# Attention with a mixture of experts: last half batch reordered, gathers issued eight pairs ahead

## The reference

```python
x = L0_attn_x                                    # 4 x 1024 x 256, float32
x = x + layernorm(attention(layernorm(x)))       # 16 heads, 4 kv heads, rotary, causal
x = x + layernorm(ffn(layernorm(x)))
# ffn(x): 64 experts of width 96, 6 of them for each token
scores = sigmoid(x @ gate_w)                     # choice: best 4 of 8 groups, then best 6 experts
w      = scores[chosen] / sum(scores[chosen]) * 2.5
# each expert takes its first 128 * 6 * 2 * 2 / 64 = 48 tokens at most
routed = sum over chosen e of w * ((silu(x @ w_gate[e]) * (x @ w_up[e])) @ w_down[e])
shared = (silu(x @ ws_gate) * (x @ ws_up)) @ ws_down
ffn    = routed + shared
```

## Time and profile before

| | |
|---|---|
| time, median of 3 runs | 2049.85 us (2048.86 to 2051.9) |
| the profiled execution's own time | 2050.17 us |
| its span, first to last instruction | 2048.4 us |
| block `attention`, to | 1781 us of the span |
| block `last_quad`, from and to | 1781 to 1847.2 us |
| block `experts`, from and to | 1847.2 to 2048.4 us |
| PE, DVE, ACT, POOL busy over the span | 93, 65, 56, 63 per cent |

### The profile page before, as it was taken

One profiled execution on the slowest core, in us unless ns is written; L12 is line 12 of the kernel. 1 busy time (PEld: TensorE's weight loads), 2 busy tenths in 40 slices (PEclk: granted clock), 3 DMA queues, 4 the chain that ended last, 5 costly groups with the idle time before them and its releaser, 6 DMA issues. The chain is left out here.

```text
span 2048.4 us, 34361 instructions
## 1 busy us (share of the span) xinstructions
PE 1895.5 (93%) x11846; PEld 1566.2 (76%) x11846; DVE 1330.8 (65%) x3149; ACT 1154.0 (56%) x2632; POOL 1284.4 (63%) x1061
## 2 busy tenths in 40 slices
PE   5999999999999999999999999999999999787926
PEld 4888888888888888888888888888888888543412
DVE  5566666667767677777667667676676778762324
ACT  3556666666656665566565665666655655333413
POOL 5758576666666765758485766676666755214733
PEclk8999999999999999999999999999999999995658
DMA  5005000001110100000100100001101000298476
GB/s 178 16 27 164 29 21 6 22 6 31 48 52 6 42 1 22 11 27 32 58 21 6 42 6 27 6 21 57 32 6 42 1 17 17 105 357 284 67 220 210
DMA packets 77292, 120.22 MB, mean 59 GB/s; under 512 B 9639, under 2 KB 57717, under 8 KB 75873
## 3 DMA queue, kind: packets, MB, share of 16 engines
q1 hardware_dynamic: 65264, 92.61, 13.6%
q0 software_dynamic: 7248, 12.72, 2.6%
q10 hardware_dynamic: 4608, 12.68, 1.9%
HBM read 90.34 MB, written 38.53 MB: 63 GB/s over the span
## 5 line engine op out<-in xcount | busy, mean ns | idle before, releaser
L561 PE MATMUL s_ps<-kT,q 128*128 128x512 f32 (+3 forms) x2304 | 584.3, 371 | 13.9 <-POOL q L1136 7.9
L824 DVE TENSOR_TENSOR pT<-t_ps,pT 128x512 fp32r<-128x512 f32 (+3 forms) x768 | 401.0, 550 | 191.0 <-ACT pT L969 189.8
L811 DVE TENSOR_REDUCE neg_max<-s_ps 128x1 f32<-128x640 f32 (+7 forms) x512 | 384.6, 751 | 110.8 <-PE s_ps L561 103.9
L561 PEld LDWEIGHTS s_ps<-kT,q 128*128 128x128 f32 x2304 | 408.3, 192 | 61.6 <-ACT probs L958 11.6
L586 PE MATMUL av_ps<-pT,v 128*128 128x512 f32 x1728 | 442.2, 400 | 2.7 <-DVE pT L824 2.7
L1121 POOL TENSOR_TENSOR k_roped<-raw,sinT 64x512 f32<-64x512 f32 x316 | 406.7, 1287 | 24.3
L969 ACT ACTIVATE pT<-t_ps 128x512 fp32r<-128x512 f32 (+3 forms) x768 | 348.7, 490 | 129.8 <-PE t_ps L571 125.0
L958 ACT ACTIVATE probs<-s_ps,neg_max 128x640 f32<-128x640 f32 (+7 forms) x512 | 381.9, 746 | 63.3 <-DVE neg_max L811 61.0
L586 PEld LDWEIGHTS av_ps<-pT,v 128*128 128x128 f32 x1728 | 311.8, 189 | 67.1 <-DVE pT L824 7.8
L571 PE MATMUL t_ps<-k_ident,probs 128*128 128x128 f32 x2304 | 340.1, 274 | 11.6 <-DVE pT L824 7.9
L1118 POOL TENSOR_TENSOR k_roped<-raw,cosT 128x512 f32<-128x512 f32 x158 | 204.4, 1294 | 220.1 <-ACT raw L930 201.3
(11 more groups left out here) (245 smaller groups left out, 1877.4 us busy)
## 6 DMA issues: line engine op xcount, KB each, us to landing
w_early<-in_expert_w SPq DMA_DIRECT2D x5, 2560.0 KB, 26.6
w_early<-sums SPq DMA_DIRECT2D x24, 512.0 KB, 8.8
k_staged<-in_wpack SPq DMA_DIRECT2D x47, 256.0 KB, 2.9
sums<-sums ACTq DMA_DIRECT2D x2, 4144.0 KB, 22.9
k_staged<-in_wpack SPq DMA_DIRECT2D x16, 512.0 KB, 3.7
e_w_late<-in_expert_w SPq DMA_DIRECT2D x3, 2560.0 KB
k_xw<-in_x SPq DMA_DIRECT2D x4, 1024.0 KB, 5.8
k_xb<-in_x SPq DMA_DIRECT2D x4, 1024.0 KB, 5.9
```

Source lines behind the costliest of these rows:

```text
L561: last = pe.matmul(out, q[:, macro % 2, a, h, int(big)], kT[:, g % 2, s, lo:hi], start=(n == 0), stop=(n == 2))
L811: dve.reduce_max(neg_max[:, r % 16:r % 16 + 1], s_ps[:, r % 2, 0:(row_tile(r) + 1) * P], AX.X, negate=True).then_inc(max_ready, 1)
L824: dve.tensor_tensor(lo, t_ps[n % 2][:, 0:count * P].rearrange("p (j n) -> p j n", n=P), hi.bitcast(F32), ALU.subtract).then_inc(t_lo, 1)
```

## The change

There are four edits in `last_quad` and one in `experts`.
- DVE: the two instructions of `shared(0)` are taken apart (`shared_gate(0)` before the wait for the first inverse root, `shared_up(0)` after the second statistics), `shared(1)` moves from the third early round to just behind it, and the four instructions that make the weights move from behind the last round to ahead of the late rounds. On PE `down(0)` goes ahead of `transpose_x2`, on ACT `gate_tanh(1)` ahead of `x1_apply`.
- POOL: the memset of `gathered` moves from the start of the block to behind the stores of `x2`.
- `LEAD` goes from 6 to 8, which is `RING`: eight gathers are issued in the block of the lists, and g(j + 8) stands ahead of s(j) in the loop.
- The wait for `y_out` leaves the end of ACT's stream. SP waits for it at the start of the next block, ahead of the loads of `w_late`, and POOL ahead of s(0).

```diff
 class Index:
-    RING, LEAD = 8, 6
+    RING, LEAD = 8, 8
...
+            down(0)
             transpose_x2()
-            down(0)
             logits()
...
             gate_tanh(0)
+            gate_tanh(1)
             x1_apply()
-            gate_tanh(1)
...
-            for i in range(2):
-                act.wait_ge(y_out[i], 32 * B)
-
...
             store_weights(LAST - 1)
-            link(pool.memset(index.gathered[:], 0.0))
             pool.wait_ge(mv_done, 1)
...
                 pool.dma_start(token_rows(rows, LAST, t, slice(0, HID)), xw[:, t:t + 2]).then_inc(stored, 16)
+            link(pool.memset(index.gathered[:], 0.0))
             pool.wait_ge(weight_done, 1)
...
             dve.memset(last_rows[:], 0.0)
+            shared_gate(0)
             dve.wait_ge(rstd_done, 1)
...
             stats(xb, kept.x1_mv)
-            shared(0)
+            shared_up(0)
+            shared(1)
             dve.wait_ge(rstd_done, 2)
...
                 largest(kept.first, early, i)
-                if i == 2:
-                    shared(1)
...
             shared(3)

+            link(dve.tensor_tensor(kept.spare[:], kept.score[:], kept.picked[:], ALU.mult))
+            link(dve.tensor_reduce(kept.weight_sum[:], kept.spare[:], AX.X, ALU.add))
+            link(dve.reciprocal(kept.weight_inv[:], kept.weight_sum[:]))
+            dve.tensor_tensor(kept.row_w[:, LAST % 2], kept.spare[:], kept.weight_inv[:].unsqueeze(2).broadcast_to([P, 4, EXPERTS]),
+                              ALU.mult).then_inc(weight_done, 1)
+
             dve.wait_ge(key_in, 1)
...
         @block.sync
         def _(sp):
+            for i in range(2):
+                sp.wait_ge(y_out[i], 32 * B)
...
+                if j == 0:
+                    for i in range(2):
+                        pool.wait_ge(y_out[i], 32 * B)
                 pool.wait_ge(y_odd, j + 1)
```

More of the change, by code:

```diff
@@ L1284, in __init__, with last_quad @@
         self.from_row, self.to_row = sb("from_row", [P, EXPERTS // 2], I32), sb("to_row", [P, EXPERTS // 2], I32)
-def last_quad(nc, consts, kept, index, rows, x1_rows, x2t_rows, y_rows, w_early, w_in, shared_in, gathered_in):
+def last_quad(nc, consts, kept, index, rows, x1_rows, x2t_rows, y_rows, w_early, w_in, shared_in, gathered_in, y_out):
     with ExitStack() as ctx:
@@ L1319, in last_quad @@
         gate_ready, up_ready, tanh_done, a_done, h_done = (sem(n) for n in ("gate_ready", "up_ready", "tanh_done", "a_done", "h_done"))
-        down_ready, y_read, y_out = sem("down_ready"), sem("y_read"), [sem(f"y_out{i}") for i in range(2)]
+        down_ready, y_read = sem("down_ready"), sem("y_read")
         block = ctx.enter_context(nc.Block())
@@ L1531, in stats, with shared_gate, shared_up @@
                 last.then_inc(mv_done, 1)
-            def shared(n):
+            def shared_gate(n):
                 dve.wait_ge(tanh_done, n + 1)
                 dve.scalar_tensor_tensor(a[:, n % 2], th[:, n % 2], 1.0, gate_ps[n % 2][0:FF], ALU.add, ALU.mult).then_inc(a_done, 1)
+            def shared_up(n):
                 dve.wait_ge(a_done, n + 1)
@@ L1540, in shared @@
                 dve.scalar_tensor_tensor(h[:, n % 2], a[:, n % 2], 0.5, up_ps[n % 2][0:FF], ALU.mult, ALU.mult).then_inc(h_done, 1)
+            def shared(n):
+                shared_gate(n)
+                shared_up(n)
             def largest(at, left, i):
@@ L1604, in _ @@
             dve.sem_inc(largest_done, 1)
[L1606 to L1610, removed]
             dve.wait_ge(turned, 2)
@@ L1619, in _, with experts @@
             shared(7)
-def experts(nc, consts, kept, rows, index, w_early, w_in, gathered_in, sums, x1_rows, out):
+def experts(nc, consts, kept, rows, index, w_early, w_in, gathered_in, sums, x1_rows, y_out, out):
     with ExitStack() as ctx:
@@ L1929, in build @@
         gathered_in = [ctx.enter_context(nc.semaphore(f"gathered_in{i}")) for i in range(index.RING)]
-        last_quad(nc, args, kept, index, rows, x1_rows, x2t_rows, sums[0:TABLE], w_early, w_in, shared_in, gathered_in)
-        experts(nc, args, kept, rows, index, w_early, w_in, gathered_in, sums, x1_rows, out)
+        y_out = [ctx.enter_context(nc.semaphore(f"y_out{i}")) for i in range(2)]
+        last_quad(nc, args, kept, index, rows, x1_rows, x2t_rows, sums[0:TABLE], w_early, w_in, shared_in, gathered_in, y_out)
+        experts(nc, args, kept, rows, index, w_early, w_in, gathered_in, sums, x1_rows, y_out, out)
 def lay_out(inputs):
```

## The result

The changed kernel takes 2042.80 us (median of 8 runs, 2040.19 to 2046.18), the kernel before 2049.65 in the same session (8 runs, 2048.85 to 2051.90): ratio 0.9966, 95% interval 0.9956 to 0.9976, so 6.9 us faster. The prediction was 2043.5, with a range of 2038.5 to 2049.5. The profiled execution shown here took 2044.19, its span 2042.2.

A forecast was written before the change was run, and what follows sets the result against it. The bound was when s(27) lands, with `experts` started by POOL's drain and a fixed tail behind. Gains of 2.8 to s(8), 2.2 to s(23) and 1.4 to s(27) sum to 6.4 us: 2043.5 us, range 2038.5 to 2049.5.

The forecast's parts named there:

- The drain beyond the last gather: End of the block of the lists: POOL's drain outlasts its last gather by 3.1 us, so `experts` starts at 1842.4.
- that edit is worth 2.3 of the 4.9: Start of `experts`: taking the wait for `y_out` off ACT gives 2.3 of the 4.9 us gained there.
- The four even steps: Loop, s(0) to s(8), scatters under load: steps of 9.05, 9.05, some 10 and 7.5 us; s(8) at 1888.4, 2.8 earlier.
- the ends, 1878.8 and 1899.2: Bounds for s(8) in the loop: issue alone gives 1878.8, four steps of 11.6 us give 1899.2.
- nothing in the rows shows a step of 8: Loop, even chain: the argument against scatter steps of 8 us, which would put s(8) at 1884.8.
- the second rival, More: Loop: steps of 8 us or PE's higher level put s(8) 6.4 earlier; 10 us in all, 2040.2; chance 0.17.
- the 2.2: Loop, s(8) to s(23): gain of 2.2 us, 48.7 for 50.9, as earlier gathers keep PE from holding POOL.
- 91.4 us behind it: From s(27)'s landing to the end: a stretch taken as untouched by the change, 91.4 us.
- Slower: Loop: every even step 11.58 us as two loads join; 4.3 us slower, 2054.5; decides from 10.5 on; chance 0.09.
- Less: Loop steps of 10 us, s(8) at 1892.8; or block's start stays at 1847; 2047.9; chance 0.22.
- the 0.4 that I gave back: Loop, s(23) to s(27): 0.4 us off the 1.8 gained, because PE reaches y(27) at that same time.

The follow-up runs named there:

- e5: The changed kernel with ACT's wait for `y_out` put back at the end of the block of the lists: ratio 0.9963, against 0.9966 without.
- e2: The kernel before with only the four weight instructions moved ahead of the late rounds: 3.4 us faster.
- e1: The kernel before with only LEAD raised from 6 to 8: the time is the same.
- e9: The kernel before with 60 dummy matmuls on TensorE ahead of the last stage: 2046.86 us, 4.0 us faster than the kernel before.
- e6: The changed kernel with scatter j ahead of gather j + 8 in POOL's loop: the expected 2041.5 us did not come; measured time not given in the text.
- e7: The changed kernel with 100 dummy matmuls on TensorE ahead of the last stage: 3.9 us slower than the changed kernel.
- e10: The changed kernel with 60 dummy matmuls on TensorE ahead of the last stage: 2040.44 us.
- e12: The changed kernel with `w_late` and `x1` loaded in pieces and 60 dummy matmuls ahead of the last stage: 2040.22 us.
- e8: The changed kernel with `w_late` loaded in 12 pieces and `x1` in 8, each when a pair is through: 1.4 us faster.
- e3: The kernel before with only the wait for `y_out` moved from ACT to SP and POOL: the time is the same.
- e4: The changed kernel with LEAD back at 6: time not lower than the changed kernel's, nor 1 to 3 us higher.
- e11: The changed kernel with a lead of six and 60 dummy matmuls ahead of the last stage: 2040.75 us.

## Why the prediction was right

**What bounds.** Right: the meeting, the loop's scatters up to s(27), then a fixed chain of loads. Each of these moved by what the change did to it.

**The lists and the gathers.** Right within 0.2 us: residual rows 1786.2 (1786.0), first gather 1828.9 (1828.8), end of the last 1839.2 (1839.1), all less the 1.4.

**The meeting.** The drain beyond the last gather was taken as 3.1 and took 3.5: start at 1842.9 for 1842.4. The step "that edit is worth 2.3 of the 4.9", on the wait for `y_out`, was mis-sized: it measured 0.6 at the start of the block and nothing in the time (e5). It held ACT to 1844.6, which is 63.5 after the release, and POOL to 61.1; in e5 they were through at 62.3 and 62.0. There ACT's last stores were issued by 58.4, 2.0 earlier than before, and landed 3.9 later, nearly the 4.2 of before. In after they were issued by 60.2, and SP waited for them for another 0.9 us in the new block, until 2.5 after their issue; so in that execution the edit is worth about 1 us at the block's start (an estimate from these rows). What carries the gain of the block's start is the edit of the weights: alone (e2) it gives 2.4 us there and 3.4 of the 6.9 us in the time, with ACT's wait still in place. It takes the store of the weights out of the way of the first gather (50.0 after the release in e2, 55.2 before), and so also parts the gathers from ACT's last stores. The other edits in this block, which were not tried alone, bring the first gather to 47.8. The stores landed 3.9 to 4.5 us after their issue in before, e1, e5 and e9, where gathers were still being issued beside them, and 2.1 to 2.6 in e2, after, e6, e7, e10 and e12, where POOL had issued the last gather before; that the gathers are the cause is argued from this, not tested by itself. For the same reason `y_out` had come when SP issued `w_late` at 1843.8, where 1844.8 was forecast.

**The loop.** s(0) was at 1853.3 (predicted 1852.8). The four even steps took 8.74, 8.06, 10.07 and 7.88, sum 34.75, for 9.05, 9.05, 10 and 7.5, sum 35.6: s(8) at 1888.0 for 1888.4. The choice between the ends, 1878.8 and 1899.2, was right; e8 comes within 1.4 us of the lower one, issue alone, and no run shows the upper. But the sum hardly moved: before, the four steps were 9.05, 7.74, 6.49 and 11.58, together 34.86. Taking that over would have given 1887.7, and the "nothing in the rows shows a step of 8" of the second rival overlooks the two in the middle, 14.23 us from 1865.38 to 1879.61 in the earlier trace rows.

s(8) to s(23) took 48.72 for 48.7; s(23) to s(27) 9.04 for 9.4. The second is shown to be the lead's: with whole loads it is 9.0 to 9.7 in every kernel with a lead of eight, and 10.9 to 12.7 with six. The first is right in size, but its cause is open. POOL did keep 3.25 us a pair through the 24 us in which TensorE was at the lower level (clock 0.50), where before it took 3.54. With a lead of six, though, the stretch takes 50.9 and 50.8 in before and e9, at a mean granted clock of 0.61 and 0.64, and only 49.8, 49.6, 49.0 and 48.7 in e3, e2, e4 and e11, at 0.71 to 0.78; after had 0.71. So part of the 2.2, or all of it, can be TensorE's higher level in that execution, which the prediction did not foresee. No run with a lead of eight had the clock of before.

**The tail.** The "91.4 us behind it", taken as fixed, was the step with the least in it to hold. Over fourteen kernels the tail runs from 88.7 to 94.5. Leaving out e7, whose stage starts late, it follows the column "low": 88.7 to 89.1 where low is 1.9, 90.5 to 92.1 where it is 3.5 to 4.7, 93.1 to 94.2 where it is 6.6 to 6.8. It was right here by chance: before and after had 4.3 and 4.1. e4 and e6, which bring s(27) another 1.4 to 2.8 us forward, got nothing for it. That this loss is TensorE's level and not the loads is shown by the first part of the tail, table loads to last loads (1984.43 - 1951.56 = 32.9 in after), which is 32.8 to 33.9 in all, and by what is left of the stage without low, 45.7 to 46.3. Why the level falls in the middle of the stage, once or twice for 1.6 to 1.9 us in every execution but that of e7, is open; that it depends on when the stage begins is argued from e4 and e6, not shown.

**The rivals.** The times of "More" and "Slower" leave out the 0.3 between the profiled execution and the median, which the forecast takes off; nothing hangs on it. Less and more coming through were both wrong in the same place: the mean even step was 8.7, neither 10 nor 8, and the block's start did not stay at 1847. The slower one fell clear of its threshold of 10.5, with a largest step of 10.07 for the pair under the join of the two loads.

The sum, 6.4, stands beside 7.5 at s(27) and 6.9 in the medians. The 1.1 too little is 0.4 at s(8), 3.2 earlier for 2.8, and 0.8 in the last four pairs, where 11.2 became 9.0 and TensorE needed nothing of the 0.4 that I gave back.

## What to carry to other kernels

A wait for a transfer is not a fixed date: before pricing "this engine would still wait until then", ask whether the change moves the traffic that made the transfer late. Where a stage with TensorE follows a long idle time, some matmuls without use just ahead of it can be worth more than half of what a change in scheduling is (60 of them gave 4.0 us on the kernel before, 0.2%, where the change gave 6.9); count them to end before the first real one, since 100 cost more than they gave. Gains of 2 to 3 us upstream can vanish in such a stage, so read them at the last instruction that the change touches, and only then in the time.

The fastest kernels here are the changed one with 60 dummies, the same with a lead of six, and the same with the loads in pieces: 2040.44, 2040.75 and 2040.22. The three cannot be told apart, and their intervals touch that of after.

## What the hardware showed that was not expected

- TensorE stayed at the lower level for 24 us while its rows show it busy all the time: the window 1884 to 1908 of after, 24.00 of 24.00 us busy, clock 0.50. The Trainium skill, "TensorE: Matmul & The Clock Gate", Part 1, has idling as what lowers the clock and sustained work as what raises it. The start of the last stage agrees with that (2.08 us a pair after 27.55 idle, 1.02 later); this window does not. The falls in the middle of the stage each began in the first or second pair behind a short idle time, but not each such time brought one: 1.89 us stood ahead of the fall at 2001.84 in e4, and ahead of 2003.29 in after, where the level stayed.
- POOL's drain ended 3.5 us after its last gather in after, 3.1 in the earlier trace rows, 2.4 in e2, 2.9 in e10 and 4.2 in e8.
- The same code of `attention` released the next block between 1779.3 (e12) and 1783.2 us (e7) in these profiled executions. That is as large as what most edits here do, so rows of two executions are best compared from the release. From there, too, s(27) differs by up to 1.6 us where the code ahead of it is the same (164.7, 164.6 and 163.1 in after, e7 and e10), so the 1.4 us of e6 are not safe.
- Scatters beside fp32 additions of DVE took 2.59 (1963.56) and 2.16 us (1980.01) in after, as in the earlier trace rows, where the addition had started first. One at 1972.40, beside an addition that started 0.65 us after it, took the usual 1.55.
